# Eight chained layers on one core: rounding in the 8-bit gated layer moved to ScalarE, another order of head sums in the fp8 attention, a fourth stack in the last attention

## What is computed

```
x = x + L0_xattn(ln(x), ctx, ...)
x = x + L0_ffn(ln(x), ...)          # top 6 of 32 experts
x = x + L1_xattn(ln(x), ctx, ...)   # fp8 attention, heads of 128, each normed
x = x + L1_ffn(ln(x), ...)          # top 2 of 8 experts
x = x + L2_xattn(ln(x), ctx, ctx)
x = x + L2_ffn(ln(x), ...)          # 8-bit gated layer
x = x + L3_xattn(ln(x), ctx, mask, mask, ...)
x = x + L3_ffn(ln(x), ...)
```

```
aq(x)  = clip(round(x * s), -128, 127) / s,   s = 127 / max(max|x| of the row, 1e-5)
h = silu(aq(x) @ Wgate.T) * (aq(x) @ Wup.T)          # 1024 wide
h = ln_weight * h / sqrt(mean(h*h) + 1e-6)
out = aq(h) @ Wdown.T
```

## Time and profile before

| | us |
|---|---|
| median of 3 runs | 2259.33 |
| lowest, highest | 2258.38, 2268.91 |
| the profiled execution, its own time | 2274.26 |
| its span, first to last instruction | 2272.5 |
| fp8 attention (590 to 1400) | about 810 |
| gated layer (1763 to 1930) | about 167 |
| last attention, after its head (1930 to 2165) | about 235 |

### The profile page before, as it was taken

One profiled execution on the slowest core, in us unless ns is written; L12 is line 12 of the kernel. 1 busy time (PEld: TensorE's weight loads), 2 busy tenths in 40 slices (PEclk: granted clock), 3 DMA queues, 4 the chain that ended last, 5 costly groups with the idle time before them and its releaser, 6 DMA issues. The chain is left out here.

```text
span 2272.5 us, 41321 instructions
## 1 busy us (share of the span) xinstructions
PE 1915.8 (84%) x12949; PEld 1178.3 (52%) x12949; DVE 1763.4 (78%) x4155; ACT 1355.3 (60%) x3511; POOL 959.4 (42%) x1253
## 2 busy tenths in 40 slices
PE   5999889999678999999999998598588566888888
PEld 3444355666356666666666675465244133333335
DVE  4899758464579999999999988665686797888845
ACT  0777721343168888888888886132266564577753
POOL 4444200443376566665566543232874121343210
PEclk7899859999889999999999999699599776799979
DMA  6577520678230000000001001542797310577610
GB/s 147 145 179 180 129 91 1 198 246 260 73 61 20 17 20 22 20 20 22 17 20 22 10 4 47 181 139 81 206 259 201 96 35 21 134 187 184 166 39 38
DMA packets 258319, 223.63 MB, mean 98 GB/s; under 512 B 36601, under 2 KB 237916, under 8 KB 257852
## 3 DMA queue, kind: packets, MB, share of 16 engines
q1 hardware_dynamic: 234812, 179.24, 28.8%
q0 software_dynamic: 12240, 32.39, 5.5%
q10 hardware_dynamic: 11056, 9.38, 1.3%
HBM read 142.50 MB, written 79.32 MB: 98 GB/s over the span
## 5 line engine op out<-in xcount | busy, mean ns | idle before, releaser
L3579 POOL TENSOR_TENSOR f_hr<-f_hr,half_pow 128x4 f32<-128x4 f32 x192 | 215.4, 1122 | 192.1 <-DVE f_hr L3399 191.6
L966 ACT ACTIVATE a_PT<-bank 128x512 f32<-128x512 f32 x384 | 214.7, 604 | 84.5 <-PE bank L720 77.6
L852 DVE TENSOR_REDUCE a_nm<-bank 128x2 f32<-128x512 f32 x384 | 243.2, 683 | 25.6 <-PE bank L713 24.2
L3492 ACT ACTIVATE f_Pm<-bank,f_nmax 128x128 f32<-128x128 f32 x512 | 183.6, 391 | 100.0 <-DVE f_nmax L3414 99.7
L713 PE MATMUL bank<-a_stack_k,a_stack_q 57*128 57x256 bf16 (+1 forms) x768 | 165.0, 300 | 80.1 <-DVE a_nm L852 45.3
L3280 PE MATMUL bank<-f_cut_w,f_zc 128*128 128x512 f16 x768 | 202.5, 388 | 14.0 <-DVE f_raw L3409 7.8
L3573 POOL TENSOR_TENSOR f_Pm<-f_Pm,f_rs 128x512 f32<-128x512 f32 x128 | 142.6, 1114 | 111.9 <-DVE f_rs L3419 111.9
L3409 DVE TENSOR_TENSOR f_raw<-bank,f_hr 128x512 f32<-128x512 f32 x192 | 131.3, 684 | 60.1 <-POOL f_hr L3579 59.4
L966 ACT ACTIVATE f_cut_w<-bank 128x512 f32<-128x512 f32 x256 | 141.7, 600 | 51.6 <-PE bank L720 41.0
L852 DVE TENSOR_REDUCE spare<-bank 128x2 f32<-128x512 f32 x256 | 162.4, 681 | 8.8 <-PE bank L713 7.4
L720 PE MATMUL bank<-a_stack_q,a_stack_k 60*128 60x256 bf16 (+1 forms) x768 | 157.7, 290 | 4.4 <-ACT a_PT L966 4.1
(11 more groups left out here) (417 smaller groups left out, 4960.1 us busy)
## 6 DMA issues: line engine op xcount, KB each, us to landing
o<-a_sums SPq DMA_DIRECT2D x32, 512.0 KB, 4.2
cut<-a_parts SPq DMA_DIRECT2D x64, 192.0 KB, 3.9
cut<-a_parts SPq DMA_DIRECT2D x96, 128.0 KB, 3.2
m_w<-in_w SPq DMA_DIRECT2D x32, 368.0 KB, 4.6
moe_out<-m_oe ACTq DMA_DIRECT2D x32, 256.0 KB
cut<-spare SPq DMA_DIRECT2D x32, 192.0 KB, 3.5
cut<-spare SPq DMA_DIRECT2D x48, 128.0 KB, 2.6
spare<-cut SPq DMA_DIRECT2D x32, 192.0 KB, 3.6
```

The source lines that it names most:

```text
L852: v.tensor_reduce(self.nm[:, g % 2, :, at % self.J, at // self.J], self.k.bank[h % 3][:, :].rearrange("p (n m) -> p n m", n=2), AX.X, ALU. ...
L966: a.activation(self.PT[:, h % 8, :, :].rearrange("p m n -> p (m n)"), self.k.bank[3 + h % 3][:, :], ACT.Exp).then_inc(self.a_exp.sem, 1)
L3492: x = a.activation(self.Pm[:, i, j * P:(j + 1) * P], ps[:, j * P:(j + 1) * P], ACT.Exp, bias=self.nmax[:, i, j:j + 1], accum_out=self.rs[: ...
L3579: g.tensor_tensor(f, f, self.k.half_pow[:, 0:self.HPB], ALU.pow).then_inc(self.g_hr.sem, 1)
```

## The change

Gated layer: the five operations in which VectorE clips, rounds and multiplies h by the norm's weights are taken out. ScalarE adds the constant within its scaling (Identity with a bias), the integers are turned in f32, and ScalarE's copy from PSUM subtracts the constant and writes bf16; nothing is clipped. GpSimd multiplies h by the norm's weights; the norm's factor goes into the small scale values. The f32 h takes two banks (6 and 7) when turned, x takes bank 5, and so the next attention's side products go to bank 4, which the down product uses too, with waits between them; four head steps go to a step. silu's result and the bf16 copies lie in memory of the pairs' rows.

Fp8 attention: on VectorE the early sums and a rounding piece come before the scaling of late heads.

Last attention: four stacks, and the load at 24 instead of 27.

```diff
-    HEAD_BANK = 5
+    HEAD_BANK = 4
...
-        self.NST = 3 if layer != 2 else 6
+        self.NST = {0: 3, 2: 6, 3: 4}[layer]
...
     def loaded(self, t):
-        return self.starts(t, 14 if self.layer == 2 else 27)
+        return self.starts(t, {0: 27, 2: 14, 3: 24}[self.layer])
...
-    TAIL, HEAD_FROM, HEAD = 5, 7, 3
+    TAIL, HEAD_FROM, HEAD = 5, 7, 4
...
     def pe(self, t):
...
             if b_dn is not None:
+                for what, at in beside:
+                    done = (self.after.a_V, at + 1) if what == "V" else (self.after.v_m, self.after.by_dve[what, at] + 1)
+                    t.wait_ge(done[0].sem, done[0].at(done[1]))
+                beside = []
                 self.down(t, b_dn)
...
             for s in self.head(n):
+                for use in self.after.side(s):
+                    if b_dn is not None:
+                        t.wait_ge(self.v_dn.sem, self.v_dn.at(b_dn + 1))
+                    beside.append(use)
                 self.after.pe_step(t, s)
 
     def hidden_T(self, t, b):
-        t.wait_ge(self.v_hq.sem, self.v_hq.at(b + 1))
+        t.wait_ge(self.a_rh.sem, self.a_rh.at(b + 1))
         if b:
             t.wait_ge(self.a_hT.sem, self.a_hT.at(b))
-        pt = self.k.bank[7][:, :].bitcast(BF16)
+        pt = self.k.two_banks(3)
         for c_ in range(self.IC):
-            x = t.transpose(pt[:, c_ * P:(c_ + 1) * P], self.hq[:, b % 2, c_ * P:(c_ + 1) * P], self.k.ident16[:, :])
+            x = t.transpose(pt[:, c_ * P:(c_ + 1) * P], self.h[:, b % 4, c_ * P:(c_ + 1) * P], self.k.ident[:, :])
...
     def dve(self, v):
+        v.memset(self.magic[:, 0:1], TO_INT).then_inc(self.v_magic.sem, 1)
+        v.memset(self.magic[:, 1:2], -TO_INT).then_inc(self.v_magic.sem, 1)
...
-            if b_xr is not None:
-                self.to_integer(v, self.xn[:, b_xr % 2, :], b_xr, self.a_rx)
-                self.within(v, self.xn[:, b_xr % 2, :], self.xq[:, b_xr % 2, :], b_xr, self.p_xT, self.v_xq)
             if b_q is not None:
+                v.wait_ge(self.g_y.sem, self.g_y.at(b_q + 1))
                 self.largest(v, self.h[:, b_q % 4, :], b_q, 7)
...
             if b_q is not None:
-                self.inverse(v, b_q, 7, self.v_rh)
+                c.after()
+                c.mark(v.reciprocal(sc[:, b_q, 8:9], sc[:, b_q, 7:8]))
+                c.mark(v.tensor_scalar(sc[:, b_q, 9:10], sc[:, b_q, 7:8], wm[:, 2:3], 1.0 / 127.0, ALU.mult, ALU.mult))
+                c.after()
+                v.tensor_scalar(sc[:, b_q, 8:9], sc[:, b_q, 8:9], sc[:, b_q, 6:7], 127.0, ALU.mult, ALU.mult).then_inc(self.v_rh.sem, 1)
...
-            if b_hr is not None:
-                self.to_integer(v, self.h[:, b_hr % 4, :], b_hr, self.a_rh)
...
-            if b_hr is not None:
-                self.within(v, self.h[:, b_hr % 4, :], self.hq[:, b_hr % 2, :], b_hr, self.p_hT, self.v_hq)
...
-                c.mark(v.scalar_tensor_tensor(x, x, sc[:, b_nm, 6:7], self.lnw[:, :], ALU.mult, ALU.mult))
...
     def act(self, a):
...
-                a.activation(x, x, ACT.Copy, scale=sc[:, b_q, 8:9]).then_inc(self.a_rh.sem, 1)
+                a.activation(x, x, ACT.Identity, bias=self.magic[:, 0:1], scale=sc[:, b_q, 8:9]).then_inc(self.a_rh.sem, 1)
...
-                a.copy(self.hqT[:, b_hr % 2, :], self.k.bank[7][:, :].bitcast(BF16)).then_inc(self.a_hT.sem, 1)
+                a.activation(self.hqT[:, b_hr % 2, :], self.k.two_banks(3), ACT.Identity, bias=self.magic[:, 1:2]).then_inc(self.a_hT.sem, 1)
...
     def pool(self, g):
...
+                g.tensor_tensor(x, x, self.lnw[:, :], ALU.mult).then_inc(self.g_y.sem, 1)
...
             if self.on(u - 2):
                 self.sums(v, u - 2)
+            for x in self.early(w):
+                self.head_squares(v, x)
+            next(rounding, None)
             for x in late:
                 self.scale_heads(v, x)
-            next(rounding, None)
-            for x in self.early(w):
-                self.head_squares(v, x)
             next(rounding, None)
             self.prepare(v, w)
```

More of the change, by code:

```diff
@@ L2517, in allocate @@
         self.stats, self.mv = s("stats", [P, B, 6]), s("mv", [P, B, 4])
[L2518 to L2521, removed]
+        self.xqT = s("xqT", [P, 3, D], BF16)
+        self.sc, self.magic = s("sc", [P, B, 12]), s("magic", [P, 2])
+        self.h = s("h", [P, 4, I])
+        space = Space(self.before.pairs.rows.rearrange("p r j d -> p (r j d)")) if self.before else None
+        take = space.take if space else lambda shape, dt: s(f"own{shape[-1]}", shape, dt)
+        self.sil, self.hqT = take([P, 2, BANK], F32), take([P, 2, I], BF16)
         self.signals()
@@ L2641, in dve @@
             if b_q is not None:
-                self.scale(v, b_q, 7)
+                v.wait_ge(self.g_ms.sem, self.g_ms.at(b_q + 1))
+                c.after()
+                c.mark(v.tensor_scalar(sc[:, b_q, 7:8], sc[:, b_q, 7:8], sc[:, b_q, 6:7], EPS, ALU.mult, ALU.max))
             if b_hid is not None:
@@ L2663, in dve @@
                 self.largest(v, self.xn[:, b_in % 2, :], b_in, 0)
-            if b_q is not None:
-                c.mark(v.tensor_scalar(sc[:, b_q, 9:10], wm[:, 2:3], sc[:, b_q, 7:8], None, ALU.mult))
             if b_in is not None:
                 self.scale(v, b_in, 0)
-                self.inverse(v, b_in, 0, self.v_rx)
+                c.after()
                 c.mark(v.tensor_scalar(sc[:, b_in, 2:4], wm[:, 0:2], sc[:, b_in, 0:1], None, ALU.mult))
-            if b_nm is not None:
-                x = self.h[:, b_nm % 4, :]
-                if b_nm == 0:
-                    v.wait_ge(self.d_par.sem, self.d_par.at(1))
-                v.wait_ge(self.g_ms.sem, self.g_ms.at(b_nm + 1))
-                c.mark(v.scalar_tensor_tensor(x, x, sc[:, b_nm, 6:7], self.lnw[:, :], ALU.mult, ALU.mult))
+                v.reciprocal(sc[:, b_in, 1:2], sc[:, b_in, 0:1]).then_inc(self.v_rx.sem, 1)
             for t in self.tail(n):
@@ L2690, in scale @@
         self.k.dve.mark(v.tensor_scalar(m, m, EPS, 1.0 / 127.0, ALU.max, ALU.mult))
-    def inverse(self, v, b, at, done):
-        self.k.dve.after()
-        v.reciprocal(self.sc[:, b, at + 1:at + 2], self.sc[:, b, at:at + 1]).then_inc(done.sem, 1)
-    def to_integer(self, v, x, b, scaled):
-        v.wait_ge(scaled.sem, scaled.at(b + 1))
-        self.k.dve.mark(v.tensor_scalar(x, x, TO_INT, TO_INT + 127.0, ALU.add, ALU.min))
-    def within(self, v, x, dst, b, taken, done):
-        self.k.dve.after()
-        if b >= 2:
-            v.wait_ge(taken.sem, taken.at(b - 1))
-        v.tensor_scalar(dst, x, TO_INT - 128.0, TO_INT, ALU.max, ALU.subtract).then_inc(done.sem, 1)
     def product(self, v, b, n):
@@ L2720, in act @@
                     a.wait_ge(self.p_ub.sem, self.p_ub.at(2 * (b_xr - 2)))
-                a.copy(self.xqT[:, b_xr % 3, :], self.k.bank[6][:, 0:P].bitcast(BF16)).then_inc(self.a_xT.sem, 1)
+                a.activation(self.xqT[:, b_xr % 3, :], self.turned_x(), ACT.Identity, bias=self.magic[:, 1:2]).then_inc(self.a_xT.sem, 1)
             if b_q is not None:
@@ L2735, in act @@
                 a.wait_ge(self.v_rx.sem, self.v_rx.at(b_in + 1))
-                a.activation(x, x, ACT.Copy, scale=sc[:, b_in, 1:2]).then_inc(self.a_rx.sem, 1)
+                if b_in == 0:
+                    a.wait_ge(self.v_magic.sem, self.v_magic.at(2))
+                a.activation(x, x, ACT.Identity, bias=self.magic[:, 0:1], scale=sc[:, b_in, 1:2]).then_inc(self.a_rx.sem, 1)
             if b_xr is not None:
```

22 lines of the change are left out of this document (16 added, 6 removed).

## The result

The changed kernel takes 2251.9 us (median of 19 runs, 2239.6 to 2258.8), the kernel before beside it 2261.8 (19 runs, 2256.8 to 2274.9). The ratio is 0.9934, 95% interval 0.9916 to 0.9952: 15 us faster, between 11 and 19. (The two medians are 9.9 us apart, the two means 14.3.) The forecast was 32 us; the time lies within the range given, the gain is about half of the forecast or less. The profiled execution after has a span of 2253.4 us, against 2272.5.

What follows compares the result with a forecast made beforehand. VectorE was taken to pace the gated layer's ten steps and the fp8 attention. Gains of 14 (gated layer), 18 (fp8 attention) and 0 (stacks) sum to 32 us, from the median 2259.3 to 2227 us, range 2190 to 2254.

Steps and rivals of the forecast that it cites:

- Gated layer ... 14 us gained: Gated layer: 8 us in ten steady steps, 5 at the end, 3 before, less 2 for bank 4.
- the 2 us for bank 4: Gated layer: TensorE's new waits before the down product in five steps, 2 us lost, between 0 and 7.
- ScalarE's ring: Gated layer: ScalarE's own work plus its wait for TensorE's answer, 7.0 us a step at full clock.
- Rival A: Gated layer: TensorE's clock stays about 0.70, steady steps lose 6 us, total 2241; chance 0.18 together with Rival E.
- What VectorE loses to it ... I take nothing: Gated layer: GpSimd's new product costs VectorE 0 us.
- its bad end of 0.7: Gated layer: VectorE loses at worst 0.7 us a step (11 us) to GpSimd's new product.
- Rival E: Gated layer: one VectorE scaling a step waits out GpSimd's product, 2.3 us; total 2241; chance 0.18 together with Rival A.
- 0.69 us gained ... 0.40 us of new idle. Per pair 0.29; 64 pairs give 18 us: Fp8 attention: late-head steps gain 0.69 us, the other steps lose 0.40, 18 us gained in all.
- The prediction's own sign: Fp8 attention: new idle before L3406 on f_sq of about 25 us in all; more would mean Rival B.
- three of the four pairs of a batch read like the one shown: Fp8 attention: argument against Rival B, that the step pair read from the trace stands for three of four.
- Rival B: Fp8 attention: square too late in late-head steps also, no gain, 0.40 us loss stays, +26 us, total 2271; chance 0.07.
- Four stacks ... I take 0: Last attention: TensorE's stall goes but VectorE's maxima cover it, 0 us gained, at most 12.

Runs made afterwards that it cites:

- e10: Kernel before with one rounding piece moved ahead of the late heads' scaling in the fp8 attention; ratio 0.9872 to the kernel before, attention 714.7 us.
- e9: Changed kernel with the rounding piece moved ahead of the early sums in late-head steps of the fp8 attention, scaling still last; 2215.3 us, ratio 0.9798.

## Why the prediction was wrong, point by point

- **"Gated layer ... 14 us gained": the number is right, 13.2 in the profile, 12 alone; the step behind it is right in part, and two errors in it largely cancelled.** By its parts: the last ten full steps 92.8 to 86.5 us, 6.3 (forecast 8); the first five 1.9 (3); from the last b_stats to the last add 43.1 to 38.1 us, 5.0 (5); the 2 us for bank 4 are within these. The prediction expected VectorE at 5.5 us a step, with gaps, and ScalarE's ring at 7.0 at full clock. The plain step fell from 8.18 to 6.53 us, beneath that 7.0, and VectorE has no gap in it: 5.5 us and 1.0 of L2678 held up. The ring was too long because its 5.2 us of ScalarE are a mean over ten steps with the next attention's work in them; in the plain step ScalarE is busy 3.26 us. The steps that carry head steps went from about 9.2 to 10.4, which I had not seen; there VectorE does wait for TensorE, as the ring says. The clock over the ten steps went to 0.78, not 0.88. Rival A is out: it gave the layer no gain.
- **"What VectorE loses to it ... I take nothing": wrong by 0.45 us a step on the mean,** inside its bad end of 0.7, and by 1.0 us in the plain step, where it set the length. Rival E's mechanism was there in four of ten steps. VectorE's L2678 and GpSimd's product, changed kernel:

```profile
1841.32 1.42 DVE L2678 TENSOR_SCALAR a_sums<-X,b_mv 128x256 f32<-128x256 f32 x1
```

```profile
1840.24 2.35 POOL L2770 TENSOR_TENSOR b_h<-b_h,a_sums 128x1024 f32<-128x1024 f32 x1
```

  The first ends at 1842.74, the second at 1842.59: the scaling, 0.40 us by itself, stood until GpSimd was nearly through. The Trainium skill ("SBUF — State Buffer", Who interferes with whom) calls the port pair that VectorE and GpSimd share an exclusive lock, held for a whole instruction; here the trace agrees, for this operation. VectorE's operation out of PSUM in the same 2.35 us (L2671, 0.47 us at 1840.93) was not lengthened.
- **The row that the prediction rested this on says the same.** It read L2698 at 1862.08, 1.48 us, as "not one held up for all of GpSimd's work". GpSimd's product beside it in the same trace (L1073, 128x512) began at 1861.86 and lasted 1.15 us. It ends at 1863.01, and L2698, 0.76 us on the mean, at 1863.56: that fits an operation held until GpSimd was through and then done. That the scalings left are short was no reason for nothing, as what is lost is the rest of GpSimd's instruction and not a share of one's own. Rival E's price was off too: its 8.3 us hold 0.5 of the next stage's work, so they stand against the 9.2 of the ten steps and not against the plain step's 8.2, and are 9 us gained in the ten steps instead of next to nothing.
- **"0.69 us gained ... 0.40 us of new idle. Per pair 0.29; 64 pairs give 18 us": this step failed.** The loss was there, 0.30, 0.32, 0.10 and 0.31 us in the four steps of a batch without late heads. The gain was read off one late-head step and carried to four. Step 7, the one shown, gained 0.65 as forecast. Step 3 gained 0.27: the sums came sooner, but the rounding piece behind them then met GpSimd's division and took 1.22 us on the mean, where it had taken 0.65. Steps 1 and 5 gained 0.08 and 0.01. Sum: 1.01 gained, 1.03 lost in a batch, nothing. The prediction's own sign said so: it looked for about 25 us of new idle before L3406 and wrote that more means B; it was 51.9.
- Steps 1 and 5 could have been read blind. In the kernel before, ScalarE and then VectorE in step 1 of a batch:

```profile
1092.01 0.71 ACT L3527 ACTIVATE f_sq<-bank 128x512 f32<-128x512 f32 x1
```

```profile
1092.73 0.69 DVE L3409 TENSOR_TENSOR f_raw<-bank,f_hr 128x512 f32<-128x512 f32 x1 [0.89 <-POOL f_hr L3579]
```

  The square ends at 1092.72, just when GpSimd's factors are there: putting the one wait in place of the other buys 0.01 us. Over 12 batches it ended 0.01 us ahead in step 1, 0.72 in step 3, nothing in step 5. In step 7 it ended 0.69 us ahead. **"three of the four pairs of a batch read like the one shown"** was the false sentence; one does, and a second does until GpSimd comes in.
- Step 3's piece beside GpSimd's division, changed kernel:

```profile
1101.91 1.30 DVE L3440 TENSOR_TENSOR f_cs<-f_cb,f_cm 128x512 bf16<-128x512 bf16 x1
```

```profile
1101.88 1.04 POOL L3580 TENSOR_TENSOR f_Pm<-f_Pm,f_rs 128x512 f32<-128x512 f32 x1
```

- **Rival B named the mechanism** (ScalarE must first square the heads of the step before) but priced it as all or nothing, +26 us, at 0.07. It held in two of four late-head steps, and the sum was the zero between the two cases. A case at 2245 was missing from the list.
- **What I did not ask:** what VectorE could do in the idle time. Whether it waits for the factors or for the square, the rest of the step follows the wait. The change moved a wait and left both pieces behind it in late-head steps. One piece ahead of it (e10) gives the kernel before some 30 us.
- **"Four stacks ... I take 0": right.** The transfers' waits went and the length stayed. That VectorE's maxima cover the stall is argued in the prediction; no run tests it by itself.

## What to carry to other kernels

When an engine waits in every round for one of two results, do not ask only which comes first; ask what ready work stands behind the wait that could stand ahead of it. Here that was worth some 30 us, more than a third of them because the piece also got clear of GpSimd's division (0.65 us long behind the wait, 0.42 ahead of it), and the choice between the two waits nothing. And when a loop's rounds differ, read the time of arrival in each kind of round before multiplying one of them: four rows instead of one (two steps with 0.7 us to gain, two with none, and 0.40 to lose in each of the other four) would have put the fp8 term near zero. Work moved to GpSimd is not free for a VectorE that has no slack: in the plain step it took 1.13 us off VectorE and cost it 1.01. Try it on both.

## What the runs showed of the hardware

- VectorE's scaling of 128x256 f32 in SBUF lasted 1.42 us instead of 0.40, and a bf16 sum of 128x512 1.30 instead of 0.41, each ending 0.1 to 0.3 us after the GpSimd product that ran beside it. In the changed kernel's step 7 the two began 0.01 us apart (1080.27 and 1080.28): there the bf16 sum took 0.41 us and GpSimd's division 1.31 instead of 1.03.
- On GpSimd a product of 128x1024 f32 took 2.35 us, on VectorE 1.21.
- ScalarE's copy of 128x1024 out of PSUM took 1.11 us in f32 with a bias, 1.00 in bf16 without one.
- The same kernel's runs spread over 20 to 30 us. The fp8 attention repeated within about 1 us; the time to the first f_nmax varied by 17 (632.2 to 649.0) between kernels that do not differ there (granted clock over the first 630 us 0.89 in the kernel before, 0.91 in e9), and the last attention's tail by 4.
